# Row gathers on GpSimd, with the loads of column numbers and the stores of rows on SyncE and the stores of expert outputs on ScalarE

## The reference

```python
def _forward(x, edge_index, W_gat, att_src, att_dst, b_gat, ln_gamma, ln_beta, W1, b1, W2, b2):
    h = (x_flat @ W_gat).reshape(M, HEADS, NUM_EXPERTS)
    src = jnp.concatenate([edge_index[0], loops])
    dst = jnp.concatenate([edge_index[1], loops])
    a_src = (h * att_src).sum(-1)
    a_dst = (h * att_dst).sum(-1)
    e = jax.nn.leaky_relu(a_src[src] + a_dst[dst], negative_slope=0.2)
    e_max = jax.ops.segment_max(e, dst, num_segments=M)
    ee = jnp.exp(e - e_max[dst])
    denom = jax.ops.segment_sum(ee, dst, num_segments=M)
    alpha = ee / (denom[dst] + 1e-16)
    msg = h[src] * alpha[:, :, None]
    agg = jax.ops.segment_sum(msg, dst, num_segments=M).reshape(M, HEADS * NUM_EXPERTS) + b_gat
    scores = _layernorm(agg, ln_gamma, ln_beta).reshape(M, HEADS, NUM_EXPERTS).mean(1)
    topk_s, topk_i = jax.lax.top_k(scores, TOP_K)
    w = jax.nn.softmax(topk_s, axis=-1)
    for ei in range(NUM_EXPERTS):
        g = jnp.where(topk_i == ei, w, 0.0).sum(-1)
        hh = jax.nn.gelu(x @ W1[ei] + b1[ei], approximate=False)
        out = out + g[..., None] * (hh @ W2[ei] + b2[ei])
    return out
```

## Time and profile before

| | |
|---|---|
| median of 3 runs | 3535.85 us (3533.83 to 3540.76) |
| the profiled execution | 3530.0 us |
| its span in the trace | 3528.4 us |
| PE busy | 2313.8 us, 66% |
| POOL busy | 1818.5 us, 52% |
| DVE busy | 1779.4 us, 50% |
| ACT busy | 629.2 us, 18% |
| mean granted TensorE clock | 0.84 of full speed |

### The profile page before, as it was taken

The page is one execution under the profiler, slowest core; times in us unless marked ns, Lnnn a source line. Parts: engine busy times, 40 slices in busy tenths (PEclk is TensorE's granted clock), DMA queues, the critical chain, the costliest instruction groups (busy, mean ns, idle before and its releaser), DMA issues. The chain is left out here.

```text
span 3528.4 us, 36268 instructions
## 1 busy us (share of the span) xinstructions
PE 2313.8 (66%) x11702; PEld 1769.9 (50%) x11702; DVE 1779.4 (50%) x3556; ACT 629.2 (18%) x837; POOL 1818.5 (52%) x1886
## 2 busy tenths in 40 slices
PE   2888888888885868888888849999999400000000
PEld 2777777777774555656655526666666300000000
DVE  8666666666663458988999920000000000003897
ACT  1122222222222322222322211212212100000000
POOL 0777777777771002232312337777777777773310
PEclk8899999999998988999998969999999755555555
DMA  5644444444443240010101042222222211115315
GB/s 197 210 132 132 131 130 131 132 132 131 129 132 125 74 131 25 24 48 30 43 24 48 17 81 63 63 69 57 65 63 63 41 15 15 15 17 195 103 54 201
DMA packets 178583, 307.54 MB, mean 87 GB/s; under 512 B 41427, under 2 KB 119890, under 8 KB 176726
## 3 DMA queue, kind: packets, MB, share of 16 engines
q0 software_dynamic: 70816, 136.49, 16.1%
q1 hardware_dynamic: 79002, 132.29, 11.6%
q10 hardware_dynamic: 28700, 37.99, 3.3%
HBM read 228.82 MB, written 77.81 MB: 87 GB/s over the span
## 5 line engine op out<-in xcount | busy, mean ns | idle before, releaser
L1896 POOL DMA_INDIRECT er<-row_dram,gi x832 | 787.3, 946 | 279.3 <-issue 237.7
L396 POOL DMA_INDIRECT xg<-xn_dram,gidx x784 | 741.3, 945 | 239.6 <-issue 233.3
L420 PE MATMUL ps_e<-we,eaT 65*128 65x256 f32 x1568 | 410.2, 407 | 79.0 <-DVE msg L543 70.3
L439 PEld LDWEIGHTS ps_a<-inwin,msg 128*128 128x128 f32 x3136 | 413.4, 205 | 17.4 <-ACT msg L463 5.1
L439 PE MATMUL ps_a<-inwin,msg 128*128 128x128 f32 x3136 | 412.6, 288 | 4.7 <-ACT msg L463 4.7
L2017 DVE TENSOR_TENSOR eo<-ps_en,eb_r 128x1024 f32<-128x1024 f32 (+1 forms) x52 | 60.5, 1163 | 657.0 <-PE ps_en L1968 657.0
L1350 POOL TENSOR_SCALAR hg<-hg,mv,rs 128x256 f32<-128x256 f32 x49 | 99.8, 2046 | 553.5 <-DVE rs L1120 553.5
L543 DVE TENSOR_TENSOR msg<-ps_e,xg 128x1024 f32<-128x1024 f32 x196 | 238.8, 1219 | 279.7 <-DMA xg<-xn_dram,gidx 279.7
L1959 PE MATMUL ps_em<-xT,ew 128*128 128x512 f32 (+1 forms) x832 | 345.5, 571 | 40.3 <-DMA xT<-x3T_dram 40.3
L420 PEld LDWEIGHTS ps_e<-we,eaT 65*128 65x128 f32 x1568 | 295.5, 198 | 144.6 <-DVE msg L543 101.5
L463 ACT ACTIVATE msg<-msg 128x1024 f32<-128x1024 f32 x196 | 207.1, 1057 | 796.0 <-DVE msg L543 763.6
(11 more groups left out here) (284 smaller groups left out, 2595.4 us busy)
## 6 DMA issues: line engine op xcount, KB each, us to landing
eaT<-in_eaT SPq DMA_DIRECT2D x98, 256.0 KB
eo_dram<-eo SPq DMA_DIRECT2D x48, 512.0 KB, 2.9
eo<-eo_dram SPq DMA_DIRECT2D x12, 2048.0 KB, 10.5
er<-row_dram,gi POOLq DMA_INDIRECT x832, 2.4
xg<-xn_dram,gidx POOLq DMA_INDIRECT x784, 2.7
xm<-xm_dram SPq DMA_DIRECT2D x24, 512.0 KB, 4.0
erow<-none ACTq DMA_DIRECT2D x1, 10240.0 KB, 36.3
erow<-er POOLq DMA_DIRECT2D x52, 160.0 KB, 2.1
```

The lines of the kernel that those rows point to most:

```text
L396: pool.indirect_dma_start(xg[:, q, b, :], None, M["xn_dram"], bass.IndirectOffsetOnAxis(ap=gidx[:, q, b:b + 1], axis=0)).then_inc(s_g[q][b ...
L420: t = pe.matmul(ps_e[h][:, b * D:(b + 1) * D], eaT[:, q, h * HB + b, :], we[:, :], start=True, stop=True)
L439: t = pe.matmul(ps_a[:, q, c * P:(c + 1) * P], msg[:, q, b, c * P:(c + 1) * P], inwin[:, q, b, :], start=False, stop=False, skip_group_che ...
L1896: pool.indirect_dma_start(er[:, r, b, :], None, M["row_dram"], bass.IndirectOffsetOnAxis(ap=gi[:, r, b:b + 1], axis=0)).then_inc(s_get[r], 16)
```

## The change

GpSimd's stream in `gat_edges_and_experts` keeps only the gathers. The tile `order_sb` goes, with its load and the copies from it. SyncE now loads each batch's 128 x 16 column numbers straight into `gi` by a DMA (four before the weights, and then one behind each store, for the batch four further on) and stores the gathered rows. SyncE's former work, the stores of `eo`, goes to ScalarE: the store of expert e - 1 stands behind the GELUs of expert e, and the last one behind the last GELU, ahead of the next group's `xT` load.

```diff
-        order = sb("order_sb", [P, S3, MB], I32)
...
+        def batches(eng):
+            reach = nc.values_load(M["reach"][0:1, 0:1], engines=[eng.engine], min_val=R * P * MB, max_val=E2 - 1)
+            return reach // (R * P * MB)
+
         with nc.Block() as block:
             @block.gpsimd
             def _(pool):
-                def stage(j, r):
-
+                def gather(j, r):
+
+                    pool.wait_ge(s_idx[r], j * 16 + 16)
+                    pool.sem_inc(s_go, 1)
                     pool.wait_ge(s_put[r], j * 16)
-                    nc.gpsimd.tensor_copy(gi[:, r, :], order[:, j * R + r, :]).then_inc(s_idx[r], 1)
-
-                def gather(j, r):
-                    pool.wait_ge(s_idx[r], j + 1)
                     pool.sem_inc(s_go, 1)
                     for b in range(MB):
                         pool.indirect_dma_start(er[:, r, b, :], None, M["row_dram"],
                                                 bass.IndirectOffsetOnAxis(ap=gi[:, r, b:b + 1], axis=0)).then_inc(s_get[r], 16)
 
-                def store(j, r):
-
-                    pool.wait_ge(s_get[r], j * (16 * MB) + 16 * MB)
-                    pool.dma_start(M["erow"][bass.ds((j * R + r) * (P * MB * ROWC), P * MB * ROWC), :].rearrange("(p n) o -> p (n o)", p=P),
-                                   er[:, r, :, :].rearrange("p b c -> p (b c)")).then_inc(s_put[r], 16)
-
-                pool.dma_start(order[:, :, :], M["order"].rearrange("(s p b) o -> p s (b o)", p=P, b=MB)).then_inc(s_ord, 16)
-                pool.wait_ge(s_ord, 16)
...
+                last = batches(pool)
                 with pool.Fori(0, last) as j:
                     for r in range(R):
-                        n, m = (j, r + 1) if r + 1 < R else (j + 1, 0)
-                        stage(n, m)
-                        gather(n, m)
-                        store(j, r)
+                        gather(j, r)
...
             @block.sync
             def _(sp):
+                def list_of(j, r):
+                    sp.dma_start(gi[:, r, :], M["order"][bass.ds((j * R + r) * (P * MB), P * MB), :].rearrange("(p b) o -> p (b o)", p=P)).then_inc(s_idx[r], 16)
+
+                def store(j, r):
+
+                    sp.wait_ge(s_get[r], j * (16 * MB) + 16 * MB)
+                    sp.dma_start(M["erow"][bass.ds((j * R + r) * (P * MB * ROWC), P * MB * ROWC), :].rearrange("(p n) o -> p (n o)", p=P),
+                                 er[:, r, :, :].rearrange("p b c -> p (b c)")).then_inc(s_put[r], 16)
+
+                for r in range(R):
+                    list_of(0, r)
...
-                def store(j, b, T):
-                    i = j * 2 + b
-                    for e in range(NE):
-                        sp.wait_ge(s_e, i * NE + (e + 1))
-                        sp.dma_start(M["eo_dram"][:, bass.ds(i * G, T), e, :],
-                                     eo[:, e % 2, 0:T, :]).then_inc(s_st[e % 2], 16)
-
-                over_groups(sp, store)
...
+                last = batches(sp)
+                with sp.Fori(0, last) as j:
+                    for r in range(R):
+                        store(j, r)
+                        list_of(j + 1, r)
+                for r in range(R):
+                    store(last, r)
+                for r in range(R):
+                    sp.wait_ge(s_put[r], 16 * (last + 1))
+                    sp.sem_inc(s_end, 1)
...
+                        if e:
+                            store(i, e - 1, T)
+                    store(i, NE - 1, T)
+
+                def store(i, e, T):
+
+                    act.wait_ge(s_e, i * NE + (e + 1))
+                    act.dma_start(M["eo_dram"][:, bass.ds(i * G, T), e, :], eo[:, e % 2, 0:T, :]).then_inc(s_st[e % 2], 16)
 
                 over_groups(act, group)
+                for b in range(2):
+                    act.wait_ge(s_st[b], 16 * (NE // 2) * (NG + 1))
```

More of the change, by code:

```diff
@@ L1873, in gat_edges_and_experts @@
         s_put = [sem(f"s_put{r}") for r in range(R)]
-        s_ord = sem("s_ord")
+        s_end = sem("s_end4")
         s_go = sem("s_go4")
@@ L1897, in gather @@
                                                 bass.IndirectOffsetOnAxis(ap=gi[:, r, b:b + 1], axis=0)).then_inc(s_get[r], 16)
-                def store(j, r):
-                    pool.wait_ge(s_get[r], j * (16 * MB) + 16 * MB)
-                    pool.dma_start(M["erow"][bass.ds((j * R + r) * (P * MB * ROWC), P * MB * ROWC), :].rearrange("(p n) o -> p (n o)", p=P),
-                                   er[:, r, :, :].rearrange("p b c -> p (b c)")).then_inc(s_put[r], 16)
-                pool.dma_start(order[:, :, :], M["order"].rearrange("(s p b) o -> p s (b o)", p=P, b=MB)).then_inc(s_ord, 16)
-                pool.wait_ge(s_ord, 16)
[L1908 to L1911, removed]
+                last = batches(pool)
                 with pool.Fori(0, last) as j:
                     for r in range(R):
-                        n, m = (j, r + 1) if r + 1 < R else (j + 1, 0)
-                        stage(n, m)
-                        gather(n, m)
-                        store(j, r)
+                        gather(j, r)
                 for r in range(R):
[L1919 to L1924, removed]
+                    gather(last, r)
             @block.sync
             def _(sp):
+                def list_of(j, r):
[6 more added lines that the diff above has]
+                    list_of(0, r)
                 for e in range(NE):
@@ L1932, in _ @@
                 sp.dma_start(b1[:, :], A["eb1"]).then_inc(s_w, 16)
-                def store(j, b, T):
-                    i = j * 2 + b
-                    for e in range(NE):
-                        sp.wait_ge(s_e, i * NE + (e + 1))
-                        sp.dma_start(M["eo_dram"][:, bass.ds(i * G, T), e, :],
-                                     eo[:, e % 2, 0:T, :]).then_inc(s_st[e % 2], 16)
-                over_groups(sp, store)
-                for b in range(2):
-                    sp.wait_ge(s_st[b], 16 * (NE // 2) * (NG + 1))
+                last = batches(sp)
[8 more added lines that the diff above has]
+                    sp.sem_inc(s_end, 1)
             @block.tensor
```

## The result

The changed kernel takes 3452.47 us (median of 4 runs, 3451.11 to 3454.71), beside 3536.18 us (3533.83 to 3540.76, 4 runs) for the kernel before: a ratio of 0.9764, 95% interval 0.9748 to 0.9779, or 83.7 us less. The profiled execution took 3451.11 us with a span of 3449.4 us, the one of before 3530.0 with 3528.4. The mean granted clock is 0.85, before 0.84.

The account below looks back on a forecast made before the run. The prediction took GpSimd's stream of gathers to bound the stage, with 430 us of cover over the experts. Gains of 68.3, 14.7 and 0.4, together 83.4 us off the median, gave 3452.5 us, range 3447 to 3484.

Parts of the forecast that it names:

- The joints: Between gather batches on GpSimd: without store and copy, 51 joints shrink from 2.59 to 1.25 us, gaining 68.3 us.
- The start: At the stage's start: a small first list in place of the whole 512 KB lets gathers begin 14.7 us earlier.
- The end: From last gather to next stage: SyncE's last store issues and lands quicker than GpSimd's, gaining 0.4 us.
- The experts: At 12 group joints TensorE idles 72 us for `xT`, plus 30 of slow clock, all covered by the gathers.
- The rival of the waits: At each batch joint the gather with two waits pays 0.49 us more, 25.0 in all: 3477.5 us; chance 0.11.
- The rival of the late first list: At the stage's start the first list lands as late as the big one, no gain: 3467.2 us; chance 0.08.
- The rival of the experts as the bound: In the experts the clock stays low through each group, so they outlast the gathers: about 3843 us; chance 0.03.

Follow-up runs that it names:

- the store alone: Changed kernel with only the row stores put back on GpSimd, lists still loaded by SyncE: 3478.40 us, ratio 0.9845.
- the copy alone: Changed kernel with the list again loaded whole and copied batch by batch by GpSimd, stores still on SyncE: 3512.29 us, ratio 0.9946.
- four small buffers: Changed kernel with four buffers of 8 x 128 rows in place of 16 x 128, and `xT` loaded ahead of the stores: 3401.29 us, ratio 0.963.
- the long loop: Changed kernel with two buffers of 16 x 128 and the loop body written twice, 64 gathers a round, 832 in all: 3453.68 us, ratio 0.9782.
- the last experiment: Changed kernel with four buffers of 4 x 128 and `xT` ahead, on a slower chip: 4278.59 us beside 4491.7 for the kernel before, ratio 0.9517.
- small-batch kernels: Changed kernel with two buffers of 8 x 128 rows in place of four of 16 x 128, and `xT` ahead: 3398.76 us, ratio 0.9626.

## Why the prediction was right, and where it wasn't

- **Total.** 3452.5 was predicted and 3452.47 measured, in the range. The agreement to 0.03 us is luck. The sum was taken from two executions' positions against their medians: before's profile lay 5.9 us below its median, after's 1.4. The same kernel gave 3448.4 when it was run again. By ratio, 0.9764 and 0.9767 stand beside 3452.5 / 3535.85 = 0.9764 predicted.
- **The joints (68.3).** 65.7 in the traces. The mechanism is exact: a joint is a plain step with its 0.30 of idle. What is missing is 831 x 0.0026 = 2.2 us by the level of the gather in this execution; in the run with 944 ns the gain is 1105.4 - 1037.5 = 67.9. The runs with the store alone (0.60 at each joint) and the copy alone (0.71) add up to 1.31, beside 1.34 predicted and 67.9 / 51 = 1.33 measured; it is shown by two runs that the gain is the sum of both, and which part brought which.
- **The start (14.7).** 15.5. The 8 KB lists landed quicker than a gather's 2.4, in 1.8, and the 0.3 for the load of the batch count, which no row had shown, added nothing: 1.8 and the 0.88 of the earlier trace rows make nearly all of the 2.76. Measured from the stage's first issue, the first gather came 2.76 us later, where 3.6 was predicted.
- **The end (0.4).** 0.5, with a step missing, so that the agreement is luck. The prediction had the landing, the store, its landing and the barrier. What it left out is the drain of GpSimd's sequencer, which ended last in both kernels. Before, it came behind the store's landing. In the changed kernel it began ahead of the last gathers, and SyncE had been done for 5.7 us when it ended, so that the cheaper issue and landing of the store, from which the 0.4 was made, were not on the path. The size itself repeats: from the last gather's start to the next stage it is 11.96 us before and 11.91 with the store back on GpSimd, and 11.45 in both executions of the changed kernel and with `xT` ahead. But small changes elsewhere moved it to 5.1, 5.3 and 6.0 (four small buffers, two buffers, the long loop). In the first two the drain was short enough for SyncE's own end, as predicted, to come last. The Trainium skill (DMA: Bandwidth & Descriptors, Specifications) gives the SyncE path about 0.6 us to the first byte and the GpSimd path about 1; the stores' landings agree in direction, 1.8 us now for 2.1 before, and in the changed kernel the landing doesn't set the end.
- **The experts (72 + 30, costed at nothing).** Costed rightly, sized too low. The idle time at a joint was 6.8 us and not 6, in two pieces that the timeline shows: `xT` starts 0.98 us behind the store's issue, of which the store takes 0.38 and 0.6 are unexplained by the rows, and its matmul follows 4.78 us behind the issue, for 4.15 taken from before. The second is the load itself. It lands in 4.8 us where it stands right behind a store of 512 KB (the changed kernel; 4.9 with half of the gathers) and in 4.0 or 4.1 where it doesn't (before, and both kernels with `xT` ahead). The slow restart at the joint shown is 32 matmuls in 16.2 us for 13.9, so 2.3; over the first 11 joints it is 2.6 in the mean, for 2.5 predicted. The pauses make 82 us for 72 and the restarts 30 for 30, and the last matmul came 114 us later for 102. There were 227 us of cover for 230. The run with `xT` ahead shows that all of it was covered, and the pair with half of the gathers that it would cost 111.8 us otherwise.
- **The rival of the waits (0.49 each).** Refuted: 831 idle times of 0.305 on average leave no room for one of 0.79 at every 16th. But one buffer shows where waits do cost, 4.6 us each.
- **The rival of the late first list.** Refuted: 2.76 us, with the expert weights issued behind it.
- **The rival of the experts as the bound.** Refuted for this chip: the granted clock is 0.50, 0.97 and 1.00 in the three stretches of 5 us behind a pause, and 0.94 over the whole of the experts. The Trainium skill (TensorE: Matmul & The Clock Gate, Loop structure matters more than you think) warns of a load waited for between matmuls; the trace agrees that the first matmuls behind the wait run at the lower level, and here it is 2.3 us of a group's 65. On the chip of the last experiment the experts were the bound: they went on past the gathers even with `xT` ahead, at a granted clock of 0.62 and at 122 us and more for a group, beyond the twice 55 that the clock alone could make. The changed kernel wasn't run there, so what its pauses would cost on such a chip is open.

## To carry to other kernels

Where one engine issues one DMA behind the other, count every instruction between two of them at its duration, and at the extra gap as well if the next DMA depends on it: here 0.60 for a store and 0.71 for a copy of 0.21. A wait put on such an engine is free only as long as what it waits for is done by then: here with one batch of 10 us or more between, not with none. So look at the number of buffers before the wait is called free. And when a prediction comes out to the microsecond, still compare its terms one by one: here the end and the two-buffer run were right by errors that cancelled.

## What had not been expected of the hardware

- **GpSimd's drain.** At a block's end, behind a stream of indirect DMAs, the drain of GpSimd's sequencer ended this long after the last GpSimd DMA's end: 7.5 us before and with the store back on GpSimd, where that DMA is a store; 9.2 in both executions of the changed kernel and in the copy, `xT` and small-batch kernels, 8.7 with one buffer, 4.7 with four tiny ones, 4.0 in the long-loop kernel and the two with half of the gathers, 2.8 in the four-small and 2.3 in the two-buffer kernel. What sets it wasn't found.
- **Gaps in the gathers.** 2 us at every 112th gather with two buffers (and a few of 3), 3.2 to 4.0 at every 113th with one, 1.5 at every 80th with four buffers and the copy, some of 2 with four buffers of 4 x 128 on the slow chip, none in the changed kernel nor with four buffers of 8 x 128. Neither loop length nor the number of buffers alone sorts them; the cause is open.
- **A load behind a store.** `xT` (512 KB) lands 0.8 us later when ScalarE issues it right behind a 512 KB store, 4.8 for 4.0.
- **The level of a gather.** 944 or 947 ns in the same program by execution, which is 2 to 3 us in each stage of some 800 gathers.
